# Experts stage of a post-norm attention and soft mixture kernel: two buffers of mixed rows, the first sequence's finishing in third steps, row statistics ahead of the first logits, the running maximum behind the next maximum

## What is computed

```python
x = _layernorm(x + _L0_attn_ref(...), axis=-1)       # x: 2 sequences x 1024 rows x 256
x = _layernorm(x + _L0_ffn_ref(...), axis=-1)

# _L0_ffn_ref: B=2, N=1024, D=256, E=16 experts, S=128 slots each, H=64
x_ln = (x - mean) / jnp.sqrt(var + LN_EPS) * gamma + beta
x_n = _l2norm(x_ln, -1) * scale
logits = jnp.einsum('bnd,des->bnes', x_n, _l2norm(mu, 0))
dispatch = jax.nn.softmax(logits, axis=1)                       # over the rows
combine = jax.nn.softmax(logits.reshape(B, N, E * S), axis=-1)  # over all slots
slot_in = jnp.einsum('bnd,bnes->besd', x_ln, dispatch)
h = jax.nn.gelu(jnp.einsum('besd,edh->besh', slot_in, W1) + b1, approximate=False)
slot_out = jnp.einsum('besh,ehd->besd', h, W2) + b2
out = jnp.einsum('bsd,bns->bnd', slot_out.reshape(B, E * S, D), combine)
```

## Times and profile before

| what | value |
|---|---|
| median of 3 executions | 1222.25 us (1220.8 to 1222.49) |
| profiled execution, its own time | 1219.74 us |
| its span, first to last instruction | 1217.9 us |
| mean granted TensorE clock | 0.984 of full speed |
| PE busy over the span | 1141.2 us (94%) |
| DVE, ACT, POOL busy over the span | 811.7, 790.7, 710.9 us |

### The profile page before, as it was taken

How to read it: one execution, slowest core, us unless ns; L and a number is a source line. 1 busy time by engine, 2 the same in 40 slices (tenths; PEclk the granted TensorE clock), 3 DMA queues, 4 the chain that set the end, 5 groups by cost and what they waited for, 6 DMA issues and landing times. The chain is left out here.

```text
span 1217.9 us, 23566 instructions
## 1 busy us (share of the span) xinstructions
PE 1141.2 (94%) x8096; PEld 1048.8 (86%) x8096; DVE 811.7 (67%) x1899; ACT 790.7 (65%) x1654; POOL 710.9 (58%) x485
## 2 busy tenths in 40 slices
PE   4899999999989999999989999999899989888997
PEld 3798999898989998999989989998778879787986
DVE  5565676566677567666666756776776666776677
ACT  2666676665666667778667766664588777455664
POOL 2767667667675765786757675630178635534541
PEclk9999999999999999999999999999999999989999
DMA  3331211112211112111211111200101010000101
GB/s 99 83 108 45 56 33 44 31 29 54 50 27 32 44 38 51 44 32 27 49 46 38 31 45 36 49 6 19 36 22 31 23 31 19 18 23 14 48 15 36
DMA packets 48789, 47.57 MB, mean 39 GB/s; under 512 B 13080, under 2 KB 43288, under 8 KB 48416
## 3 DMA queue, kind: packets, MB, share of 16 engines
q1 hardware_dynamic: 48384, 45.99, 14.6%
q10 hardware_dynamic: 288, 0.07, 0.0%
HBM read 24.03 MB, written 2.10 MB: 21 GB/s over the span
## 5 line engine op out<-in xcount | busy, mean ns | idle before, releaser
L536 PE MATMUL ring<-kT,qT 128*128 128x384 f32 (+5 forms) x1152 | 245.7, 349 | 9.8 <-ACT exps L701 3.9
L701 ACT ACTIVATE exps<-ring,neg_max 128x128 f32<-128x128 f32 (+7 forms) x256 | 189.2, 742 | 61.4 <-DVE neg_max L845 60.7
L845 DVE CUSTOM_DVE_ANT_0 ring<-ring,hidden 128x128 f32<-128x128 f32 (+7 forms) x256 | 191.4, 767 | 34.0 <-PE ring L536 33.3
L536 PEld LDWEIGHTS ring<-kT,qT 128*128 128x128 f32 x1152 | 186.3, 190 | 22.6 <-issue 5.4
L718 ACT ACTIVATE exp_parts<-turned 128x512 fp32r<-128x512 f32 x192 | 114.4, 596 | 134.9 <-PE turned L551 113.0
L551 PE MATMUL turned<-ident,exps 128*128 128x128 f32 x1152 | 178.7, 273 | 8.6 <-DVE exp_parts L863 4.5
L572 PE MATMUL mix<-exp_parts,v_parts 128*128 128x256 f32 x1152 | 183.8, 295 | 0.4 <-DVE exp_parts L863 0.4
L551 PEld LDWEIGHTS turned<-ident,exps 128*128 128x128 f32 x1152 | 141.6, 141 | 26.7 <-issue 7.4
L863 DVE TENSOR_TENSOR exp_parts<-turned,exp_parts 128x512 fp32r<-128x512 f32 x192 | 131.7, 686 | 33.2 <-ACT exp_parts L718 33.1
L973 POOL TENSOR_TENSOR cos_part<-taken,cos_sb 128x1024 f32<-128x1024 f32 x38 | 91.3, 2402 | 99.6 <-ACT taken L669 99.6
L572 PEld LDWEIGHTS mix<-exp_parts,v_parts 128*128 128x128 f32 x1152 | 148.8, 189 | 0.6 <-DVE exp_parts L863 0.6
(11 more groups left out here) (224 smaller groups left out, 2182.9 us busy)
## 6 DMA issues: line engine op xcount, KB each, us to landing
rotated<-taken SPq DMA_DIRECT2D x76, 256.0 KB, 3.7
raw_q<-in_L_attn_Wq_dram SPq DMA_DIRECT2D x32, 128.0 KB, 3.6
...
```

What stands on the lines that cost most here:

```text
L536: last = nc.tensor.matmul(ring_cols(item, half * BANK, piece), qT[:, H % QUERIES, a, i * P:(i + 1) * P], kT[:, G % 2, m, half * piece:(hal ...
L701: nc.scalar.activation(dst, tile, ACT.Exp, bias=neg_max[:, H % 2, i:i + 1], scale=-1.0, accum_out=row_sum[:, H % 2, i:i + 1]).then_inc(don ...
L845: nc.vector.tensor_tensor_reduce(tile, tile, later, -1.0, 3.0e38, ALU.add, ALU.min, neg_max[:, H % 2, i:i + 1]).then_inc(done[kind], 1)
```

## The change

Five things, all in the experts stage; the attention before it is as it was.

1. `mixed` gets a buffer for each sequence, and the wait of the first `combine` of sequence 1 for `vary_3` goes.
2. Sequence 0's finishing moves: row tiles 0, 1, 2 after step 18, tiles 3, 4, 5 after step 22, tiles 6, 7 with `vary_3` after step 26; `std_3` to step 28, `inv_3` to step 29; all eight `normal_a` and both stores after step 30.
3. Sequence 1's statistics: all `stats`, `vary`, `std_1`, `inv_1`, `std_2` come ahead of the first `logits`, and `inv_2`, `offsets` ahead of the first `top`. `length` moves from step 11 behind `gelu` of step 12.
4. `run` of a step at place 0 or 1 moves from ahead of the next `top` to behind it.
5. The last `fold` (i = 3) of units 3 and 7 moves from step 11 or 27 into step 13 or 29, ahead of `output`; its `folded_b` behind `top` and `run` there. `turn_unit` 2, 3 (and `unit_lo`) of sequence 1 move ahead of `spread` 2, 3 (and their `combine`) in step 14.

```diff
     def deviations(b):
-        put(*[(kind, b) for kind in ("vary", "std_1", "inv_1", "std_2", "inv_2", "offsets")])
+        put(*[(kind, b) for kind in ("vary", "std_1", "inv_1", "std_2")])
...
         put(("logits", g), *[("fold", u, i) for i in range(4)])
-        put(("top", g), (taker(0), u, 0), ("exp", g), (taker(1), u, 1), ("keep", g), (taker(2), u, 2))
+        if g == 0:
+            put((taker(0), u, 0))
+            if sequences > 1:
+                put(("inv_2", 1), ("offsets", 1))
+        put(("top", g))
+        if g:
+            put((taker(0), u, 0))
+        put(("exp", g), (taker(1), u, 1), ("keep", g), (taker(2), u, 2))
...
+    if sequences > 1:
+        moments(1, range(8))
+        deviations(1)
     begin(0)
...
-        if s == experts + 8 and sequences > 1:
-            put(("std_3", 0, 0), ("inv_3", 0, 0))
+        if s == experts + 12 and sequences > 1:
+            put(("std_3", 0, 0))
+        if s == experts - 4 and sequences > 1:
+            put(("length", 1))
         if ahead and not change:
             put(("logits", s + 1))
         if ripe and j == 1 and unfolded:
-            put(("output", v, 1))
+            put(("fold", u, 3), ("output", v, 1))
...
         if ahead and not change:
             put(("top", s + 1))
+        if s and j < 2 and live and not changed:
+            put(("run", s))
         if ripe and j == 1 and unfolded:
+            put((taker(3), u, 3))
             slots(v, 1)
...
                 fold(u + 1, 2)
-                fold(u + 1, 3)
+                if u % 4 != 2:
+                    fold(u + 1, 3)
...
         if ahead and not change:
-            put(("run", s + 1), ("inverse", s + 1))
+            if j in (1, 2):
+                put(("run", s + 1))
+            put(("inverse", s + 1))
...
+        if s == experts - 2 and sequences > 1:
+            turn_units(1, (2, 3))
         if j == 2:
             spread(v, (2, 3))
...
-            finish(0, {experts + 2: (0,), experts + 3: (1, 2), experts + 4: (3, 4, 5), experts + 5: (6, 7)}.get(s, ()))
-        if s in (experts + 10, experts + 11) and sequences > 1:
-            put(*[("normal_a", 0, 4 * (s - experts - 10) + t) for t in range(4)], ("store", 0, s - experts - 10))
+            finish(0, {experts + 2: (0, 1, 2), experts + 6: (3, 4, 5), experts + 10: (6, 7)}.get(s, ()))
+            if s == experts + 10:
+                put(("vary_3", 0, 0))
+            if s == experts + 13:
+                put(("inv_3", 0, 0))
+            if s == experts + 14:
+                put(*[("normal_a", 0, t) for t in range(8)], ("store", 0, 0), ("store", 0, 1))
...
-        mixed = sb("mixed2", [P, TILES, WIDE])
+        mixed = sb("mixed2", [P, B, TILES, WIDE])
...
                     if v % PER == 0:
-                        if v:
-                            dve.wait_ge(done["vary_3"], count("vary_3", v // PER - 1, 0))
-                        nc.vector.tensor_copy(mixed[:, t, :], spread_ps[:, t % 2, 0:WIDE]).then_inc(done[kind], 1)
+                        nc.vector.tensor_copy(mixed[:, b, t, :], spread_ps[:, t % 2, 0:WIDE]).then_inc(done[kind], 1)
```

More of the change, by code:

```diff
@@ L1060, in early @@
             return
-        if s == 2:
-            deviations(1)
         for j in {6: (0,), 7: (1, 2), 10: (3,)}.get(s, ()):
@@ L1066, in early @@
             put(("squares", 1, j))
-        if s == 11:
-            put(("length", 1))
         if s == 12:
@@ L1087, in plan_experts @@
         unfolded = live and u % 4 == 3
-        if s == experts + 6 and sequences > 1:
-            put(("vary_3", 0, 0))
         if changed:
@@ L1121, in plan_experts @@
             split_mu(s + 3)
-        if s in (0, 1, 2) and sequences > 1:
-            moments(1, ((0, 1), (2, 3, 4), (5, 6, 7))[s])
         if s == experts - 2 and sequences > 1:
@@ L1191, in plan_experts @@
                     put(("output", v, 1))
-        if s == experts - 2 and sequences > 1:
-            turn_units(1, (2, 3))
         if s + 4 < total:
@@ L1917, in _ @@
                     dve.wait_ge(done["spread"], count("spread", v, t))
+                    b = v // PER
                     if v % PER == 0:
-                        if v:
-                            dve.wait_ge(done["vary_3"], count("vary_3", v // PER - 1, 0))
-                        nc.vector.tensor_copy(mixed[:, t, :], spread_ps[:, t % 2, 0:WIDE]).then_inc(done[kind], 1)
+                        nc.vector.tensor_copy(mixed[:, b, t, :], spread_ps[:, t % 2, 0:WIDE]).then_inc(done[kind], 1)
                     else:
@@ L1924, in _ @@
                         dve.wait_ge(done["combine"], count("combine", v - 1, t))
-                        nc.vector.scalar_tensor_tensor(mixed[:, t, :], mixed[:, t, :], fade[:, v % 2, t:t + 1], spread_ps[:, t % 2, 0:WIDE],
+                        nc.vector.scalar_tensor_tensor(mixed[:, b, t, :], mixed[:, b, t, :], fade[:, v % 2, t:t + 1], spread_ps[:, t % 2, 0:WIDE],
                                                        ALU.mult, ALU.add).then_inc(done[kind], 1)
@@ L1930, in _ @@
                     dve.wait_ge(done["combine"], count("combine", b * PER + PER - 1, t))
-                    nc.vector.scalar_tensor_tensor(flat(y_row(b, t)), flat(y_row(b, t)), mixed[:, t, D:D + 1], mixed[:, t, 0:D],
+                    nc.vector.scalar_tensor_tensor(flat(y_row(b, t)), flat(y_row(b, t)), mixed[:, b, t, D:D + 1], mixed[:, b, t, 0:D],
                                                    ALU.mult, ALU.add).then_inc(done[kind], 1)
@@ L1940, in _ @@
                     ts = tiles_of(b, part)
-                    weight = mixed[:, ts, D:D + 1].rearrange("p t a -> p (t a)")
+                    weight = mixed[:, b, ts, D:D + 1].rearrange("p t a -> p (t a)")
                     settle()
```

## The result

| kernel | median (us) | runs | own time of the profiled run | its span | granted clock |
|---|---|---|---|---|---|
| before | 1222.37 | 4 (1220.8 to 1226.26) | 1219.74 | 1217.9 | 0.984 |
| changed | 1234.53 | 4 (1232.76 to 1239.02) | 1239.02 | 1237.2 | 0.981 |
| changed, second comparison | 1237.09 | 4 (1234.67 to 1237.91) | 1234.67 | 1232.9 | 0.983 |

The change made the kernel 1% slower, clear of the noise: ratio 1.0102 (95% interval 1.0075 to 1.0129), and 1.0114 (1.0099 to 1.0129) in the second comparison. Forecast was 1230.0 within 1217 to 1238.

The account below looks back on a forecast made before the run. The prediction took PE to bound the stage, so only what opens or closes PE holes counts. Its terms, from −17.6 for the finishing stalls to costs elsewhere, summed to +7.7 on the median 1222.25: 1230.0 us, range 1217 to 1238.

Parts of the forecast that it names:

- statistics, fold 3, `turn_unit`, `length`: Sequence 1's statistics ahead, the moved folds, earlier `turn_unit`, moved `length`: 5.9 − 2.1 + 4.8 + 3.0 − 2.8 us.
- The three finishing stalls and their clock: Steps 20, 22, 24: PE's three long holes and the slow matmuls behind them go, −17.6 us.
- New places and `normal_a`: Finishing in steps 18, 22, 26 costs +3.9 us; eight `normal_a` in front of `turned_a` 31 cost +2.1.
- rival C: Clock: no new hole lowers it, 1225.5 (0.09); holes in steps 12, 17, 18, 22, 28, 31 do, 1236 (0.12).
- Statistics: Ahead of the first `logits`: fold holes of 1.65 and 2.7 us, +4.4 and +1.5 for clock; −2.1 given back.
- `run`, step 4: The 1.57 us hole shrinks with `run` behind `top`: −0.65 us, between −1.8 and +0.5 with step 5.
- Fold: Steps 13 and 29: PE idles 3.8 us for `folded_b`; +2.4 a time, +4.8, and +3.0 for clock.
- `run`, place 1: Folds wait for `gathered`: holes 1.15 us in steps 21, 25, 2.15 in 17, 0.85 in 9; +5.3.
- `run`, place 0, steps 12 and 28: PE comes 1.5 us earlier, `run` falls in the third `shift`: hole 2.1 us before spread 6 twice, +4.2.
- `run`, place 0, steps 20 and 24: With step 8, from POOL's start P: `run` waits for the third `shift`; 0.55 us hole before spread 6, +1.65.
- The lock itself: A DVE instruction with two SBUF operands waits until POOL's current instruction ends, then needs about 0.95 us more.
- Rival A: Steps 8 to 28: `run` slips between POOL's instructions and takes 1.15 us; −9.3, giving 1220.7; chance 0.18.

Follow-up runs that it names:

- finish_only: The kernel before with only the change's finishing and its two `mixed` buffers; 1212.11 us, ratio 0.991.
- run_back: The changed kernel with all `run` back ahead of the next `top`; 1217.20 us, ratio 0.9951 to the kernel before.
- spread_run: The kernel before with two `mixed` buffers, finishing and `normal_a` in smaller lots, `run` of steps 4, 5 behind the next `top`; 1203.28 us, ratio 0.9839.
- nudge: The changed kernel with one 128x64 scratch copy on DVE directly ahead of `run` in steps of place 0; 1250.23 us (one run).

## Why the prediction was right, and where its sum was not

The sign came out, and the time lies in the range (1230.0 forecast, 1234.5 and 1237.1 measured), by a sum whose three blocks can now be read apart: finish_only against before, run_back against finish_only, the changed kernel (388.8) against run_back.

| block | forecast | measured |
|---|---|---|
| finishing with `normal_a` | −17.6 + 3.9 + 2.1 = −11.6 | −9.9 |
| statistics, fold 3, `turn_unit`, `length` | 5.9 − 2.1 + 4.8 + 3.0 − 2.8 = +8.8 | +5.0 |
| `run` | −0.65 + 5.85 + 5.3 = +10.5 | +18.5 |
| sum | +7.7 | +13.6 |

That the total came so near is partly luck: the block of `run` was 8.0 us too small and the finishing 1.7 too hopeful, while the block between them was 3.8 too large. The clock also blurs the split by some 1.5 us at a place: behind a hole of 1.9 us in step 19 the `gather` takes 3.11 us in finish_only and 1.97 in run_back, behind one of 2.5 us in step 31 it takes 1.97 and 3.63.

- *The three finishing stalls and their clock*, −17.6: measured −18.6. Right.
- *New places and `normal_a`*, 3.9 + 2.1: measured alone, in finish_only, 6.4 + 2.3. In the changed kernel the hole in front of `wide_inverse` 15 is 2.08 us, as the sum had it; its slow `gather` behind (1202.85, 3.56 us for 32 matmuls that take 1.97) was in rival C.
- *Statistics*: holes 1.54 and 2.36 us for the forecast 1.65 and 2.7; turn 0 5.3 us late for 5.9. Step 3 gave back the 2.1 as forecast.
- *`run`, step 4*: 0.7 us for 0.65, and it is `run` (run_back doesn't have it, spread_run does). But 1.6 us more came with it in steps 5 and 6, together 2.3, beyond the bound of 1.8: the sum had only the shorter hole and left out that the low clock behind it would go too, though the row of 4.47 us showed it.
- *Fold*: holes of 4.01 us twice for 3.8; 5.3 to 5.8 us by the turns, less what steps 11 to 14 and 27 to 30 gave back. With `run` back in its place (run_back) the holes are 2.88 us, and by the turns run_back loses only 0.2 us against finish_only in steps 11 to 14 and 1.1 in steps 27 to 30, for the forecast 4.8 + 3.0 − 2.8 = 5.0: this is where the second block was too large.
- *`run`, place 1*: steps 17, 21, 25 have holes of 2.15, 1.20, 1.21 us for 2.15, 1.15, 1.15. Step 9 has 1.99 for 0.85.
- *`run`, place 0, steps 12 and 28*: holes of 1.70 and 1.65 us for 2.1; by the turns 1.9 (3.4 in the first profile, with the clock) and 1.8.
- *`run`, place 0, steps 20 and 24: the step that failed.* "`run` starts at P + 7.0, waits for the third `shift` to end (P + 7.5)": the four last 9.47 us and not 10.4 when no DVE instruction breaks in, so the third ends at P + 7.10, and `run`, at P + 7.14, waits for the fourth. (At the P + 7.0 of the sum it would have been 0.1 us early and slipped through, so the place stood on the edge from the start.) The hole is 2.3 us for 0.55, and then the clock falls, 1.6 us more: 4.1 us by the turns instead of 0.55, twice. I had read 2.5 us for a `shift` from a row of 10.41 that held one DVE instruction's microsecond. For what `run` still needs once POOL is done I had 0.95 us; it is 1.08. So in steps 12, 20, 24 and 28 `run` took 2.65 to 3.41 us, where I had announced 2 to 2.5. Step 8 was on the lucky side (0.4), which nudge turned over.

The lock itself, the rule weighed in the prediction, is borne out by every one of these rows, and more sharply than there: the waiting time is not an average of the busy share but the rest of POOL's current instruction, from under 0.1 us (step 8) to 2.33 us (step 24). What the prediction said of DVE instructions with two SBUF operands was too narrow: nudge's copy, with one, was held too. Rival A's case (`run` slips through) was true in step 8 alone. Rival C's upper branch happened in part. Of the six steps it named, 12 (980.40) and 31 (behind 1201.25) were followed by the lower clock in the first profile, 17, 18, 22 and 28 were not, with holes of 2.15, 1.41, 1.74 and 1.65 us (those of the finishing in 18 and 22 stand in front of the next step's `peaks`); in the second profile 12 was not either. The other falls stand behind 2.36 us (857.80) and in steps 9, 13, 20, 24 and 29.
